# Two layers of a small transformer: loads of x in the first block, gates inside the second norm, experts one sequence at a time, and another order of the retention's last steps

## The reference

```
x = x + attention(layernorm(x))        # 16 heads of 8, causal
n = layernorm(x)                       # experts: gates from the first token of each sequence
g = softmax of the two largest of n[:, 0] @ Wr.T, 0 elsewhere            # 8 experts
x = x + n + sum_e g[b, e] * (n @ A[e].T) @ Bw[e].T                       # rank 64 each
n = layernorm(x)                       # retention, 4 heads, qk 32 and v 64 wide
o = (q k^T * decay) v                  # q and k rotated by position
x = x + (rmsnorm(o) * weight * silu(n @ Wg)) @ Wo
six times: x = x + window_attention(shift(x));  x = x + gated_mlp(shift(x))
```

## Time and profile before

| | us |
|---|---|
| median of three runs | 3838.73 (3838.52 to 3844.16) |
| profiled execution, whole | 3837.68 |
| its span, first to last instruction | 3835.2 |
| setup, first norm | 0 to 30.6 |
| attention | 30.9 to 340.0 |
| second norm | 340.3 to 357.7 |
| experts | 358.0 to 404.2 |
| third norm | 404.5 to 421.9 |
| retention | 422.2 to 580.0 |
| last norm | 580.3 to 603 |
| six layers | 604 to the end |

### The profile page before, as it was taken

How to read it: one execution, slowest core, us unless ns; L and a number is a source line. 1 busy time by engine, 2 the same in 40 slices (tenths; PEclk the granted TensorE clock), 3 DMA queues, 4 the chain that set the end, 5 groups by cost and what they waited for, 6 DMA issues and landing times.

```text
span 3835.2 us, 154562 instructions
## 1 busy us (share of the span) xinstructions
PE 3693.5 (96%) x61387; PEld 2330.0 (61%) x61387; DVE 3172.0 (83%) x5421; ACT 2826.4 (74%) x6426; POOL 2559.3 (67%) x2466
## 2 busy tenths in 40 slices
PE   7998888999999999999999999999999999999999
PEld 4665555666646666556666556666466665566664
DVE  6886557999968999879999789998699997799996
ACT  6895456888848888658888478888488885688883
POOL 4553226888827888648888468887388885588882
PEclk9999999999999999999999999999999999999999
DMA  2000000000000000000000000000000000000000
GB/s 79 0 0 1 1 0 2 0 6 0 1 23 2 0 6 0 1 24 0 6 0 0 24 2 0 6 0 1 24 1 0 6 0 24 2 0 6 0 1 23
DMA packets 11668, 25.62 MB, mean 7 GB/s; under 512 B 2252, under 2 KB 6392, under 8 KB 10752
## 3 DMA queue, kind: packets, MB, share of 16 engines
q1 hardware_dynamic: 11520, 23.53, 1.7%
HBM read 21.43 MB, written 2.10 MB: 6 GB/s over the span
## 4 chain that ended last, share of the span: by engine, by line
PE 80%; DVE 2%; ACT 1%; issue 1%; POOL 1%; DVEq 0%; POOLq 0%; ACTq 0%
PE banks L1124 19%; PE banks L1105 18%; PE banks L1182 9%; PE banks L1163 9%; PE banks L1113 9%; PE banks L1084 6%; PE banks L1137 5%; PE banks L1093 3%; DVE w_t L1351 1%; PE banks L1214 1%; PE banks L1072 0%; PE banks L1064 0%; PE banks L1013 0%; POOL w_t L983 0%; DVE w_ss L1391 0%
## 5 line engine op out<-in xcount | busy, mean ns | idle before, releaser
L967 POOL TENSOR_TENSOR w_t<-w_t 128x512 f32<-128x512 f32 x768 | 980.8, 1287 | 374.4 <-DVE w_t L1351 280.8
L1351 DVE TENSOR_TENSOR w_t<-banks,w_tab 128x512 f32<-128x512 f32 x1512 | 943.4, 684 | 212.6 <-ACT w_sq L1505 204.9
L983 POOL TENSOR_TENSOR w_t<-w_t,w_rn 128x512 f32<-128x512 f32 x768 | 785.1, 1044 | 257.2 <-ACT w_rn L1547 249.5
L1105 PE MATMUL banks<-w_qk,w_xs 128*128 128x512 f32 x1512 | 812.3, 619 | 0.3
L1124 PE MATMUL banks<-w_vo,w_xs 128*32 128x256 f32 x12096 | 810.7, 385 | 0.8 <-issue 0.8
L1113 PEld LDWEIGHTS banks<-ident,w_t 128*128 128x128 f32 x3072 | 380.6, 140 | 417.7 <-issue 398.6
L1498 ACT ACTIVATE w_us<-banks 128x512 f32<-128x512 f32 x756 | 450.5, 596 | 160.8 <-PE banks L1124 156.3
L1113 PE MATMUL banks<-ident,w_t 128*128 128x128 f32 x3072 | 461.2, 273 | 12.5 <-POOL w_t L983 11.6
L1391 DVE TENSOR_REDUCE w_ss<-w_sq 128x16 f32<-128x1024 f32 x378 | 457.1, 1209 | 0.0
L1124 PEld LDWEIGHTS banks<-w_vo,w_xs 128*32 128x32 f32 x12096 | 316.0, 109 | 229.4 <-issue 65.1
L990 POOL TENSOR_TENSOR w_pr<-w_pr,w_rl 128x512 f32<-128x512 f32 x384 | 403.2, 1050 | 27.2 <-ACT w_rl L1552 27.2
(11 more groups left out here) (200 smaller groups left out, 5910.7 us busy)
## 6 DMA issues: line engine op xcount, KB each, us to landing
w_qk<-w_qk_in SPq DMA_DIRECT2D x6, 1024.0 KB, 4.8
w_v<-w_v_in SPq DMA_DIRECT2D x6, 512.0 KB, 5.7
w_o<-w_o_in SPq DMA_DIRECT2D x6, 512.0 KB, 6.4
m_w<-m_w_in SPq DMA_DIRECT2D x6, 342.0 KB
xT<-x_in SPq DMA_DIRECT2D x4, 512.0 KB, 5.4
out<-kept SPq DMA_DIRECT2D x8, 256.0 KB, 2.0
m_w<-m_w_in SPq DMA_DIRECT2D x6, 171.0 KB
r_tab<-r_tab_in SPq DMA_DIRECT2D x1, 512.0 KB
```

Of the source, the lines that this page charges most:

```text
L967: nc.gpsimd.tensor_tensor(v1, v1, v2[:, :, ::-1, :], ALU.add).then_inc(S["added"], 1)
L983: nc.gpsimd.tensor_tensor(v1, v1, rn[j % 2][:, i * HALF:(i + 1) * HALF].unsqueeze(2) .broadcast_to([P, HALF, WD]), ALU.mult).then_inc(S["n ...
L1105: nc.tensor.matmul(banks[:, i, :], x[:], wqk[:, i * INNER + hh * C:i * INNER + (hh + 1) * C], start=True, stop=True).then_inc(S["qk"], 1)
L1351: nc.vector.tensor_tensor(dst[j % 2][:, i * C:(i + 1) * C].rearrange("p (h d) -> p h d", d=WD), src, tab[:, 2 * t + cs, i * WD:(i + 1) * W ...
```

## The change

The loads of x move into the setup block, ahead of everything else on SP; the increments of `COUNTED` are dealt out, a quarter each to TensorE and GpSimd and two to ScalarE. In attention each copy goes ahead of a clear. The second norm has a function of its own, `expert_norm`: beside the eight chunks it normalises the first tokens of the 16 sequences by themselves (three small products in the last chunk's bank) and makes the gates between the large operations. `experts` begins with the transpose and runs over single sequences, the scaling of sequence b + 1 beside the mix of b and the apply of b - 1. In the retention GpSimd makes the ratio ahead of the rotation's addition, TensorE the last product ahead of the head mean, ScalarE Silu and the table behind it ahead of the Square; the wait for the retention's five constants goes from the start of TensorE's list to the first weighted sum.

```diff
-        for i, b in enumerate(range(0, B, 4)):
-            sp.dma_start(xT[:, b:b + 4, PAD:], h["x"][:, b:b + 4, :]).then_inc(sem(f"x_loaded{i}"), 16)
...
+    def count(eng, part):
+        for name in COUNTED[part::4]:
+            eng.sem_inc(sem(name), 1)
...
         @block.sync
         def _(sp):
-            for name in COUNTED:
-                sp.sem_inc(sem(name), 1)
+            for i, b in enumerate(range(0, B, 4)):
+                sp.dma_start(xT[:, b:b + 4, PAD:], h["x"][:, b:b + 4, :]).then_inc(sem(f"x_loaded{i}"), 16)
             sp.sem_inc(sem("m_residual"), NCH)
+
+        @block.tensor
+        def _(pe):
+            count(pe, 0)
+
+        @block.scalar
+        def _(act):
+            count(act, 1)
+            count(act, 2)
+
+        @block.gpsimd
+        def _(pool):
+            count(pool, 3)
...
-            for i in range(2):
-                nc.gpsimd.memset(v[i][:], 0.0).then_inc(S["cleared"], 1)
...
             for b in range(2):
                 nc.gpsimd.tensor_copy(xa[b][:], norm[:, b * T:(b + 1) * T]).then_inc(S["xcopy"], 1)
+                nc.gpsimd.memset(v[b][:], 0.0).then_inc(S["cleared"], 1)
...
+            nc.tensor.matmul(banks[:, side, 0:B], mean_w[:], firsts, start=True, stop=True).then_inc(G["first_mean"], 1)
+            for c in range(NCH):
+                if c == side:
+                    pe.wait_ge(G["copied"], 1)
+                nc.tensor.matmul(of(banks[:, c, :]), mean_w[:], stream(c), start=True, stop=True).then_inc(mean_in, 1)
+                if c == 1:
+                    pe.wait_ge(G["first_squared"], 1)
+                    nc.tensor.matmul(banks[:, side, B:2 * B], mean_w[:], spread2[:], start=True, stop=True)\
+                        .then_inc(G["first_var"], 1)
+                if c >= BEHIND:
+                    variance(c - BEHIND)
+                if c == 3:
+                    pe.wait_ge(G["first_scaled"], 1)
+                    nc.tensor.matmul(banks[0:B, side, 2 * B:2 * B + E], first[:], wr[:], start=True, stop=True)\
+                        .then_inc(G["logits"], 1)
+            for c in range(NCH - BEHIND, NCH):
+                variance(c)
...
+            dve.wait_ge(G["first_mean"], 1)
+            nc.vector.tensor_tensor(first[:], firsts, banks[:, side, 0:B], ALU.subtract).then_inc(G["first_centred"], 1)
+            dve.wait_ge(G["first_centred"], 1)
+            nc.vector.tensor_tensor(spread2[:], first[:], first[:], ALU.mult).then_inc(G["first_squared"], 1)
...
+    def pipeline(eng, iteration):
+        for b in range(2):
+            iteration(b, b, lambda lag: lag <= b, True)
+        with eng.Fori(1, B // 2 - 1) as i:
+            for k in range(2):
+                iteration(i * 2 + k, k, lambda lag: True, True)
+        for b in range(B - 2, B + 1):
+            iteration(b, b % 2, lambda lag: lag >= b - B + 1, b + 1 < B)
...
+            def iteration(b, k, live, more):
+                if live(0):
                     pe.wait_ge(gated, passed(b + 1))
-                    pe.wait_ge(made, passed(i * 2))
+                    if live(2):
+                        pe.wait_ge(made, passed(b - 1))
                     for c in range(EC):
                         last = nc.tensor.matmul(banks[:, k, 0:P], ea[:, c, :], bg[k][:, c, :],
                                                 start=(c == 0), stop=(c == EC - 1))
                     last.then_inc(mixed, 1)
-                for k in range(2):
-                    b = i * 2 + k
-                    pe.wait_ge(made, passed(b + 1))
-                    pe.wait_ge(added, passed(i * 2))
-                    nc.tensor.matmul(banks[:, 2 + k, 0:T], wb[k][:], norm[:, bass.ds(b * T, T)],
+                if live(1):
+                    pe.wait_ge(made, passed(b))
+                    if live(3):
+                        pe.wait_ge(added, passed(b - 2))
+                    nc.tensor.matmul(banks[:, 3 - k, 0:T], wb[1 - k][:], norm[:, bass.ds((b - 1) * T, T)],
                                      start=True, stop=True).then_inc(applied, 1)
+            nc.tensor.transpose(banks[0:E, 5, 0:B], gates[:], ident[0:B, 0:B]).then_inc(turned, 1)
+            pe.wait_ge(turn_taken, 1)
+            for c in range(EC):
+                last = nc.tensor.matmul(banks[:, 6, c * B:(c + 1) * B], spread[:, c * P:(c + 1) * P], gT[:],
+                                        start=True, stop=True)
+            last.then_inc(spread_out, 1)
+            pipeline(pe, iteration)
...
+            def iteration(b, k, live, more):
+                if more:
+                    if live(1):
+                        dve.wait_ge(mixed, passed(b))
+                    scale(b + 1, 1 - k)
+                if live(0):
                     dve.wait_ge(mixed, passed(b + 1))
-                    dve.wait_ge(applied, passed(i * 2))
+                    if live(2):
+                        dve.wait_ge(applied, passed(b - 1))
                     nc.vector.tensor_tensor(wb[k][:], banks[:, k, 0:P], ident[:], ALU.add).then_inc(made, 1)
-                for k in range(2):
-                    b = i * 2 + k
-                    dve.wait_ge(applied, passed(b + 1))
...
+                if live(1):
+                    dve.wait_ge(applied, passed(b))
+                    rows = xT[:, bass.ds(b - 1, 1), PAD:PAD + T].rearrange("p b t -> p (b t)")
+                    nc.vector.tensor_tensor(rows, rows, banks[:, 3 - k, 0:T], ALU.add).then_inc(added, 1)
...
@@ -654,14 +789,15 @@
                     pool.wait_ge(S["g"], passed(i))
                     pool.sem_inc(sem("gate"), 1)
                     nc.gpsimd.tensor_copy(xa[:], norm[:, bass.ds(i * T, T)]).then_inc(S["xcopy"], 1)
-                    pool.wait_ge(S["taken0"], passed(i + 1))
-                    pool.wait_ge(S["taken1"], passed(i + 1))
-                    nc.gpsimd.tensor_tensor(rot[:], rot[:], rot2[:], ALU.add).then_inc(S["rotated"], 1)
                 if live(2):
                     pool.wait_ge(S["inv"], passed(i - 1))
                     pool.wait_ge(S["gtaken"], passed(i - 1))
                     pool.wait_ge(S["gated"], passed(i - 2))
                     nc.gpsimd.tensor_tensor(ratio[:], g[k][:], inverse[:], ALU.mult).then_inc(S["ratio"], 1)
+                if live(0):
+                    pool.wait_ge(S["taken0"], passed(i + 1))
+                    pool.wait_ge(S["taken1"], passed(i + 1))
+                    nc.gpsimd.tensor_tensor(rot[:], rot[:], rot2[:], ALU.add).then_inc(S["rotated"], 1)
...
                     last.then_inc(S["g"], 1)
                 if live(1):
+                    if not live(2):
+                        pe.wait_ge(S["cleared"], passed(5))
...
@@ -726,15 +864,6 @@
                                                     rot[rows, 1, t * P:(t + 1) * P], rot[rows, 0, t * P:T],
                                                     start=True, stop=True)
                     last.then_inc(S["scored"], 1)
-                if live(1):
-                    pe.wait_ge(S["squared"], passed(i))
-                    if live(0):
-                        pe.wait_ge(S["vtaken"], passed(i + 1))
-                    else:
-                        pe.wait_ge(S["logged"], passed(i - 1))
-                    pe.sem_inc(sem("gate"), 1)
-                    nc.tensor.matmul(banks[:, VB, :], head_mean[:], squares[:], start=True, stop=True)\
-                        .then_inc(S["ssq"], 1)
                 if live(2):
                     pe.wait_ge(S["gated"], passed(i - 1))
                     if live(0):
@@ -745,7 +874,15 @@
                     for c in range(2):
                         last = nc.tensor.matmul(banks[:, GB, 0:T], wo[:, c, :], oT[:, c, :], start=(c == 0), stop=(c == 1))
                     last.then_inc(S["wo"], 1)
-            pe.wait_ge(S["cleared"], passed(5))
+                if live(1):
+                    pe.wait_ge(S["squared"], passed(i))
+                    if live(0):
+                        pe.wait_ge(S["vtaken"], passed(i + 1))
+                    else:
+                        pe.wait_ge(S["logged"], passed(i - 1))
+                    pe.sem_inc(sem("gate"), 1)
+                    nc.tensor.matmul(banks[:, VB, :], head_mean[:], squares[:], start=True, stop=True)\
+                        .then_inc(S["ssq"], 1)
             pipeline(pe, iteration)
 
         @block.vector
...
                     nc.scalar.activation(v[k][:].rearrange("p t n -> p (t n)"), banks[:, VB, :], ACT.Copy)\
                         .then_inc(S["vtaken"], 1)
-                if live(1):
-                    act.wait_ge(S["evicted"], passed(i))
-                    if live(2):
-                        act.wait_ge(S["ssq"], passed(i - 1))
-                    nc.scalar.activation(squares[:], o[1 - k][:].rearrange("p a t -> p (a t)"), ACT.Square).then_inc(S["squared"], 1)
                 if live(0):
                     act.wait_ge(S["g"], passed(i + 1))
                     if live(2):
                         act.wait_ge(S["ratio"], passed(i - 1))
```

(12 more changed lines are left out.)

167 lines of the change are left out of this document (111 added, 56 removed).

## The result

| | us |
|---|---|
| before, beside it | 3839.94 (3838.52 to 3844.16, 4 runs) |
| after | 3812.3 (3808.23 to 3814.4, 4 runs) |
| ratio | 0.9926, 95% interval 0.9914 to 0.9938 |
| profiled execution after | 3811.13, span 3809.3 |

A forecast was written before the change was run, and what follows sets the result against it. TensorE bounds the six layers (3231 us, untouched); its waits in the 604 us before can shrink. 7.0 - 0.4 + 2.75 + 11.7 + 23.0 = 44.0 off 3837.7 gives 3793.7, with 1.0 for the median 3794.5; range 3787 to 3806.

The forecast's parts named there:

- Early loads: Start: x loaded ahead of SP's increments moves the first matmul from 11.93 to about 4.95, gain 7.0 us.
- the longest, at SP's price: First block: ScalarE's 54 counts, at SP's 0.061 us each, end at 4.4, before the load of x.
- rival (b): Start: counting on ScalarE, 54 increments at 0.12 us, ends the first block instead of the load; 3797 us, chance 8%.
- Attention -0.4: Attention: the first projection still waits for both clears, now behind one copy more; loss 0.4 us.
- experts 11.7: Experts: single sequences overlapped, 1.5 us each instead of 2.35; gain 11.7 us, bounds 9.3 to 13.3.
- retention 23.0: Retention: period 9.35 to 7.7 us thirteen times (21.5), plus start 0.4 and tail 1.1; gain 23.0 us.
- (a): Retention: a ring of other engines takes TensorE's place as the bound, period 8.3; 3802 us, chance 9%.
- (c): Experts: the ring doesn't overlap, each sequence pays its waits alone at 2.0 us; 3801 us, chance 6%.
- (d): Retention: drained table loads hold ScalarE's ring, period 9.7 us; 3820 us, chance 1%.
- Gates: Second norm: gates' chain removed (3.4 us), matmuls and sixteen small VectorE operations added (cost 0.65); net +2.75 us.
- The change doesn't touch them.: Six layers, from 604 us to the end: assumed to stay at 3231 us, with no gain or loss.
- Rival (e): Six layers: lower granted clock as TensorE arrives less rested; 3.2 us per 0.1%, 3849 us at 1.7%, chance 2%.

The follow-up runs named there:

- best_spread: best_0 with the first block's counting dealt to SP, ScalarE, GpSimd and VectorE: 3800.09 us.
- the traces taken again: The kernel before and the changed kernel, both unchanged, run and traced once more: 3840.49 and 3811.66 us.
- best_0: counts_off_pe plus centring 7 ahead of scaling 2, VectorE waiting for the last square before scalings 3 to 7, one attention clear on VectorE: 3797.73 us, ratio 0.9891.
- ratio_alone: Kernel before, with only GpSimd's ratio moved ahead of the addition of rot in the retention: 3830.88 us.
- pe_shifted: Changed kernel with 24 more semaphore increments on TensorE in the setup block: 3807.71 us.
- ratio_late: Changed kernel with GpSimd's addition of rot put back ahead of the ratio in the retention: 3827.5 us.
- centres_first: Changed kernel with VectorE's centrings 5 to 7 ahead of scalings 1 and 2 in the second norm, remaining gate operations between scalings: 3806.43 us.
- counts_off_pe: Changed kernel with none of the first block's counting on TensorE, ScalarE and GpSimd counting half each: 3801.49 us, ratio 0.9902.
- after_sp_placed: Changed kernel with 109 more increments on SP behind its loads: 3809.87 us.

## Why the forecast was wrong

**Early loads: +7.0, measured 6.5.** The load's 4.08 us was right (best_spread: issued at 0.75, first matmul at 4.91). The failed step is "the longest, at SP's price": I priced ScalarE's 54 counts and passed over TensorE's 28, which cost 0.152 each and end the block. It is rival (b) with another engine in it, and one of the prediction's own signs of being wrong: a matmul that waits for a block's end instead of x.

**Attention -0.4, experts 11.7, retention 23.0** held within 0.6 each, and the retention by its mechanism: both expected releases are in the rows, and each move undone gives another period. ScalarE's loads did not drain: in after a load from 419.40 lasts 1.28 and the next instruction starts at 420.70. Rivals (a), (c) and (d) are out.

**Gates: +2.75, measured +0.6** (0.4 between the traces taken again). The removed chain was right (3.7 for 3.4), the added cost of 0.65 was mis-sized: 3.1. I counted sixteen small operations at 0.2 us and VectorE's idle gaps, not what they and GpSimd do to each other. The last centring came 1.6 us late, where I had allowed 0.7; two small operations that ran into a square (0.98 and 1.05 for 0.21) lose as much. Then, with the gaps filled by products of two SBUF tiles, GpSimd's last squares found no opening, and the last one ended 3.1 late. best_0 takes 1.9 of it back.

**Last norm 0, measured -2.3.** The stage's length follows the half clock in it: 20.6 us with 2.5 us at half clock (before), 23.0 with 7.7 (after, 7 us of it at a mean clock of 0.57), 21.5 with 4.5 (ratio_alone, pe_shifted). In ratio_late and centres_first it took 20.6 as before. What decides that was not settled.

**Layers: 0, measured -14.2. The step that failed is "The change doesn't touch them."** It touches no instruction in them, but it moves their code, and of TensorE's waits on code, then of the clock, I had no term: "a layers' stage that isn't 3231 us long" was the other sign that came. Of the 14.2 us half are such waits, half is half clock (in the traces taken again, 4.2 and 7.2 of 10.3). That the place of the code moves this loss is shown among the changed kernel's variants (8 us for 10 or 22 increments more on TensorE); why the changed kernel lies worse than the kernel before is not. Rival (e) had the right place and one half of the mechanism, without its cause; at 2% and priced from 1.4% it was no help. The Trainium skill, "Runtime: NRT & Kernel Launch", section "Instruction fetch mechanics", says that code comes in 16 KiB blocks of 256 instructions and that crossing a border is "mostly hidden". Block size and trace agree (16 KB for each packet at the 149 waits); all hidden they are not: 9.0 us of waits go with them before, 16.3 after. A reader of the profile before could have seen this as a risk: the waits on issue at three lines of the layers were there.

**Open.** What sets the border's place. The number of TensorE's instructions ahead moves the waits among the changed kernel's variants (13.5 to 22.0), but the kernel before, brought to the same number on TensorE or on all engines, has 13.5 to 16.3. In the changed kernel the experts' loop, ahead of the layers, has unrolled ends that the old one had not; that such parts don't lie end to end in memory would explain it, and was not tried. Nor is it settled when a wait on code is followed by half clock: centres_first has two waits of 1.8 us or more, and only one of them is; in counts_off_pe, best_0 and best_spread a stretch at half clock begins behind two waits of only 0.4 and 0.7.

## What to carry to other kernels

When a change adds or drops instructions ahead of a long tuned stretch, allow some 10 us either way for its code lying elsewhere; compare the waits on issue before explaining a gain or loss by the edit, and try a few harmless increments. Beside a GpSimd operation that reads SBUF, give VectorE work from PSUM; filling its last gaps with two-input SBUF products stops GpSimd. Two late results in one ring are to be moved together: each alone showed about half of it or less.

## What the runs showed of the hardware

- An increment of a semaphore took 0.152 us on TensorE, by 24 of them, and 0.061 on SP; on VectorE, GpSimd and ScalarE 27 or 28 each ended before 4.83.
- A wait on issue that goes with a packet of program code lasted up to 2.5 us (after_sp_placed), while a packet took 0.9 to 1.6; from a packet's start to the next matmul it was 2.2 to 3.0 us at 149 waits.
- Half clock inside the layers began at most 4.3 us behind the start of a wait on issue, in all 33 cases.
- A 64-element VectorE operation took 0.98 us beside a square on GpSimd, 0.21 without one.
